# Loading three pairs of the last rows' matrix in two DMAs of 100 and 28 partitions

## The reference

```python
keep = (u >= P_DROP).astype(x.dtype)
x_drop = x * keep / (1.0 - P_DROP)
y = x + jnp.matmul(adj, x_drop)
m = jnp.mean(y, axis=-1, keepdims=True)
v = jnp.var(y, axis=-1, keepdims=True)
out = (y - m) / jnp.sqrt(v + 1e-05)
```

## Time and profile before

| | us |
|---|---|
| median of 3 executions | 642.21 (642.01 to 642.31) |
| profiled execution, its own time | 642.27 |
| its span, first to last instruction | 640.5 |
| TensorE busy | 514.4 (80%) |
| VectorE busy | 52.1 (8%) |
| ScalarE busy | 10.8 (2%) |
| GpSimd busy | 18.0 (3%) |

### The profile page before, as it was taken

The page is one execution under the profiler, slowest core; times in us unless marked ns, Lnnn a source line. Parts: engine busy times, 40 slices in busy tenths (PEclk is TensorE's granted clock), DMA queues, the critical chain, the costliest instruction groups (busy, mean ns, idle before and its releaser), DMA issues.

```text
span 640.5 us, 5695 instructions
## 1 busy us (share of the span) xinstructions
PE 514.4 (80%) x2308; PEld 176.1 (27%) x2308; DVE 52.1 (8%) x231; ACT 10.8 (2%) x18; POOL 18.0 (3%) x27
## 2 busy tenths in 40 slices
PE   0387797887977886887879869887887878888997
PEld 0122232232322322222222223222222222222335
DVE  3300101000010100001010010100001010000102
ACT  0000000000000000000000000000000000000000
POOL 0000000000000000000000000000000000000000
PEclk9999897988989899898889898898998888978999
DMA  9999999999999999999999999999999999999998
GB/s 391 427 435 439 429 425 443 417 438 429 434 431 456 424 434 440 430 427 443 411 443 425 430 436 452 415 450 440 426 431 437 417 443 421 434 432 434 429 421 349
DMA packets 9362, 274.83 MB, mean 429 GB/s; under 512 B 1168, under 2 KB 1424, under 8 KB 2448
## 3 DMA queue, kind: packets, MB, share of 16 engines
q1 hardware_dynamic: 9072, 274.63, 99.6%
q10 hardware_dynamic: 288, 0.16, 0.1%
HBM read 272.66 MB, written 2.13 MB: 429 GB/s over the span
## 4 chain that ended last, share of the span: by engine, by line
DMA 71%; PE 27%; issue 1%; DVE 0%; SPq 0%; POOL 0%; POOLq 0%; DVEq 0%
DMA raw<-adj_dram 71%; PE acc L162 26%; SPq L131 0%; PE turned L170 0%; POOL rstd L277 0%; PE final_acc L162 0%; DVE stats L247 0%; POOLq L45 0%; DVE rows L243 0%; SPq L134 0%; DVE moments L252 0%; POOLq L282 0%; DVE final_normed L270 0%; DVE var_eps L255 0%; DVEq L243 0%
## 5 line engine op out<-in xcount | busy, mean ns | idle before, releaser
L162 PE MATMUL acc<-raw,head 128*64 128x504 f32 x2048 | 488.1, 637 | 90.0 <-POOLq L282 89.8
L162 PEld LDWEIGHTS acc<-raw,head 128*64 128x64 f32 x2048 | 152.9, 148 | 413.5 <-issue 292.5
L243 DVE TENSOR_TENSOR rows<-turned,head 126x256 f32<-126x256 f32 x16 | 6.8, 425 | 540.1 <-PE turned L170 540.1
L277 POOL TENSOR_TENSOR rstd<-var_eps,minus_half 126x4 f32<-126x4 f32 x16 | 16.2, 1011 | 613.1 <-DMA raw<-adj_dram 394.3
L170 PE MATMUL turned<-join,sums 128*126 128x64 f32 x128 | 17.5, 279 | 10.2 <-ACT sums L219 10.2
L170 PEld LDWEIGHTS turned<-join,sums 128*126 128x126 f32 x128 | 15.3, 189 | 23.4 <-ACT sums L219 23.4
L219 ACT COPY sums<-acc 128x504 f32<-128x504 f32 x16 | 9.3, 578 | 615.7 <-PE acc L162 615.7
L258 DVE TENSOR_SCALAR normed<-rows,moments,rstd 126x64 f32 x64 | 15.7, 310 | 27.5 <-POOL rstd L277 27.5
L182 PE MATMUL final_turned<-head,eye 128*128 128x64 f32 x2 | 0.7, 448 | 21.3 <-DVE head L237 21.3
L247 DVE BATCH_NORM_STATS2 stats<-rows 126x6 f32<-126x64 f32 x64 | 9.7, 214 | 0.6
L162 PE MATMUL final_acc<-raw,head 128*64 128x128 f32 x124 | 7.7, 276 | 0.3 <-DMA raw<-adj_final_dram 0.2
(11 more groups left out here) (17 smaller groups left out, 3.5 us busy)
## 6 DMA issues: line engine op xcount, KB each, us to landing
raw<-adj_dram SPq DMA_DIRECT2D x30, 5544.0 KB, 26.7
raw<-adj_dram SPq DMA_DIRECT2D x15, 5040.0 KB, 29.2
raw<-adj_dram SPq DMA_DIRECT2D x2, 3024.0 KB, 21.2
raw<-adj_dram SPq DMA_DIRECT2D x2, 2520.0 KB, 26.8
head<-u_and_x_dram SPq DMA_DIRECT2D x1, 4128.0 KB, 13.7
raw<-adj_dram SPq DMA_DIRECT2D x1, 2016.0 KB, 20.6
out_dram<-normed SPq DMA_DIRECT2D x1, 1920.0 KB, 17.4
raw<-adj_dram SPq DMA_DIRECT2D x1, 1512.0 KB, 23.8
```

Of the source, the lines that this page charges most:

```text
L162: last = nc.tensor.matmul(sum_bank[t * D:(t + 1) * D, 0:width], dropped[:, t * PAIRS + q, :], raw[:, s, start:start + width], start=(q == ...
L243: nc.vector.tensor_tensor(rows[:, :, :], turned[0:ROWS, 0:GROUPS, :], x_sb[0:ROWS, bass.ds(b * GROUPS, GROUPS), :], ALU.add).then_inc(turn ...
L277: nc.gpsimd.tensor_tensor(rstd[:, :], var_eps[:, :], minus_half[0:ROWS, :], ALU.pow).then_inc(rstd_ready, 1)
```

## The change

The table `FINAL` is cut differently at one place: pieces 4 and 5 were of 4 and 2 pairs, (23, 27) and (27, 29), and are now of 3 and 3 pairs, (23, 26) and (26, 29). Piece 4 is loaded in two DMAs, one of partitions 0 to 99 and one of partitions 100 to 127; the first is dealt over ten queue lanes, ten rows each, and the second over fourteen, two rows each. Both add to the same semaphore, and TensorE waits for 2 x 16 on it. All else is the same.

```diff
-FINAL = [(0, 4), (4, 12), (12, 18), (18, 23), (23, 27), (27, 29), (29, 31), (31, 32)]
+FINAL = [(0, 4), (4, 12), (12, 18), (18, 23), (23, 26), (26, 29), (29, 31), (31, 32)]
+UNEVEN = 4
+UNEVEN_ROWS = [(0, 100), (100, P)]
+FINAL_DMAS = [len(UNEVEN_ROWS) if n == UNEVEN else 1 for n in range(len(FINAL))]
...
             for n, (q0, q1) in enumerate(FINAL):
-                sp.dma_start(raw[:, 0, q0 * pair:q1 * pair],
-                             adj_final[:, q0 * pair:q1 * pair]).then_inc(final_loaded[n], DMA)
+                for p0, p1 in UNEVEN_ROWS if n == UNEVEN else [(0, P)]:
+                    sp.dma_start(raw[p0:p1, 0, q0 * pair:q1 * pair],
+                                 adj_final[p0:p1, q0 * pair:q1 * pair]).then_inc(final_loaded[n], DMA)
...
                     for n, (q0, q1) in enumerate(FINAL):
-                        pe.wait_ge(final_loaded[n], DMA)
+                        pe.wait_ge(final_loaded[n], FINAL_DMAS[n] * DMA)
```

## The result

| | before | after |
|---|---|---|
| median of 13 executions, us | 642.29 (642.01 to 642.45) | 644.26 (642.96 to 644.45) |
| profiled execution, us | 642.27 | 643.29 |
| its span, us | 640.5 | 641.5 |

The change makes the kernel slower. The ratio of the times, from the means of the executions, is 1.0024 with a 95% interval of 1.0016 to 1.0032; the medians are 1.97 us apart, 0.31%. The forecast of 641.5 us missed by 2.8 us, and the range of 641.0 to 643.0 doesn't hold the median.

A forecast was written before the change was run, and what follows sets the result against it. The prediction took the kernel as a DMA-bound stream of bytes, with two late lanes delaying its end. From 642.27 us it took 0.7 for the earlier end and 0.06 for the runs' median, giving 641.5 us, range 641.0 to 643.0.

The forecast's parts named there:

- A: The forecast case: both late DMA lanes are among the six spared by the uneven deal; 641.5 us, chance 0.50.
- Relieving them: Kernel's end: late lanes' stores finish 0.69 to 0.92 us earlier, output issued 0.2 us earlier; taken as -0.7 us.
- The extra issue: SyncE's one DMA more: 1 to 3.5 us of issue hidden behind loads already in the lanes, price zero.
- TensorE's 52 weight loads: Pieces 3 to 6 run from 632.12 to 634.93 us at 54 ns a weight load, 2.81 us.
- Lanes: Piece 4's uneven deal at 0.115 us a row: ten lanes +0.46 us, four -0.69 us, two -0.92 us.
- rival C: Piece 4's ten lanes obstruct each other at half pace, losing 1.6 us; end +0.4, 642.6 us; chance alone 0.13.
- Piece 3 is unchanged, so TensorE still resumes at 632.12: TensorE's wait for piece 3 ends at 632.12 us, as before the change.
- C's signs: Pieces 4 and 5 landing after 633.2 and 633.8, lower GB/s from 631 to 634 us, long tail on many lanes.
- B: One late lane is among the ten loaded; pieces 4 to 7, stores and output move +0.46 us, 642.7 us; chance alone 0.22.
- B with C: A late lane is among the ten loaded and itself pays the half-pace cost of 1.6 us: 643.8 us; chance 0.05.
- D: Both piece 4 DMAs are dealt to all sixteen lanes, 8 or 9 rows each: 642.1 us; chance 0.10.
- -0.2 us: TensorE reaches the end of piece 6 at 634.93 in place of 635.12 us, if pieces 4 and 5 arrive in time.

The follow-up runs named there:

- f1: Kernel before with tiny loads of 10, 11, 12, 13, 14 and 16 rows ahead of the store, each awaited and copied by VectorE: 642.33 us.
- g1: Kernel before with store blocks 12 to 14 in DMAs of 100 and 28 partitions, plus tiny loads of 6 to 16 rows read by VectorE: 641.84 us.
- g2: Second execution of the kernel before with the 100 and 28 partition store end and tiny loads of 6 to 16 rows: 641.91 us.
- e2: Changed kernel, but piece 4 in two DMAs of all 128 partitions, one of two pairs and one of one: 642.35 us, ratio 1.0000.
- e1: Kernel before with only the new cut, pieces 4 and 5 of 3 and 3 pairs, piece 4 one DMA of 128 partitions: 642.29 us, ratio 0.9998.
- g3: Changed kernel with tiny loads of 6, 8, 10, 12, 13 and 16 rows ahead of the store, read by VectorE: 642.99 us.
- e3: Changed kernel, but piece 4 in two DMAs of 64 and 64 partitions: 644.08 us, ratio 1.0026 to the kernel before.
- f2: Changed kernel, but piece 4 in two DMAs of 112 and 16 partitions: 643.82 us, ratio 1.0023 to the kernel before.
- h2: Kernel before with two more stores of ten rows of 15 KB behind the others, one row a lane on lanes 0 to 9: 643.29 us.
- h3: Kernel before with two more stores of eight rows of 15 KB behind the others, on lanes 0 to 7: 643.22 us.

## Why the prediction was wrong

**What held.** The kernel is a stream of bytes and only its end moved. Two lanes are late: the probes show a step of a microsecond. They were among the six spared (A's condition) in the three profiled executions where VectorE's copies tell it (f1, g1, g2). Relieving them makes the output land 0.6 us sooner, so 0.6 of its 2.2 us was waiting behind them. The extra issue was hidden (e2). TensorE's 52 weight loads took 2.82 us where 2.81 was worked out.

**The step that failed** is "*Lanes*": "The stream runs at 429 GB/s, 26.8 per lane, so a row of 3072 B takes 0.115 us". In loads of 128 partitions (e1, e2) it comes near that, 0.125 us at the median in e1. In the load cut by partitions it didn't hold: the rows took 0.199 us at the median, and the rate fell to 261 GB/s at the same DMA share for 4 us. The ten loaded lanes were then 1.6 us later than in the store kernel (g3 against g1), not 0.46. That is rival C's figure, 1.6, though C came to it by a guess of half the pace. But C had the cost stay on the ten lanes, which were ahead. It didn't: the late lanes, still on piece 3, were slowed with them, so that TensorE resumed for piece 3 at 633.84 and not at 632.12. "Piece 3 is unchanged, so TensorE still resumes at 632.12" is the second sentence that failed, by 1.7 us. C's +0.4 should have been 0.9, which is what the lower group lies above before (643.17 against 642.29 us). C's signs came, with a lower rate between 631 and 634 us and pieces 4 and 5 landing at 634.05 and 634.89 by their last lanes in place of 633.2 and 633.8.

**B, the late lane among the loaded ones**, was priced at +0.46 over before. If the two groups are what the section before takes them for, it comes up in 7 of 13 executions and then adds 1.2 us over the same contention, and the median of 644.26 is B with C, which was put at 643.8 us and given 0.05. That is argued from times and not shown. The forecast fails without it: the lower group alone lies above the range, but for two executions just under 643.0. I had treated the late lanes as a fixed fact of the kernel, to be right or wrong once; the times speak for late lanes that differ by execution.

**D** fell: the change adds 8 signals and not the 16 that two DMAs over all sixteen lanes would add, and where the lanes keep an even share (e3, f2) the time rose as well, which D has no reason for. The "-0.2 us" of the new cut is not to be had alone (e1): its wait moves to piece 5.

## What to carry to other kernels

Don't cut a load by partitions to shift bytes between DMA lanes in a stream that keeps all of them busy. Every other deal of a load that was tried here cost time, 1.6 us with 112 and 16 partitions, where no byte was added and none had to change lanes, and it slowed the lagging lanes too. To test such an idea, read GB/s beside the DMA share in the stretch: a full share with a lower rate says that the rows themselves take longer, and a lower share is an empty queue. And look at single executions, not only at the median, when a change treats one lane unlike another: the times here suggest that what is late may not be the same lane next time.

## What the runs showed of the hardware

- A load of 384 KB cut in two by partitions goes with a lower rate in the 4 us around it, 270 (64 and 64), 328 (112 and 16) or 261 GB/s (100 and 28) in place of 419, and slows lanes that are still at work on an earlier load. I had expected a cost on the new DMAs' own lanes at most.
- The 100 and 28 cut in a store out of SBUF, at the end, shows no such cost: rows of 3 KB at 121 or 122 ns, and 641.67 to 641.86 us in the lower group. Stores of one row a lane from 8 or 10 neighbouring partitions did slow down, from 573 ns to as much as 2.0 us for a row of 15 KB (h2, h3).
- Two of sixteen lanes lag by about a microsecond, from the first load to the end. In f1 they were lanes 11 and 12; in g1 and g2, which had no probe of 11 rows, the first late one was lane 10 or 11. The times without a profiler point to another one in part of the executions.
